# Attention values one tile later than their scores, side work a tile later, and ScalarE's waits in another order

## What is computed

```python
xq = _ada_ln(x_q, t_vec, Wss_q, bss_q)
xkv = _ada_ln(x_kv, t_vec, Wss_kv, bss_kv)
q = (xq @ Wq + bq).reshape(B, Lq, nh, dh)
kv = (xkv @ Wkv + bkv).reshape(B, Lkv, 2, nh, dh)
scores = jnp.einsum('bqhd,bkhd->bhqk', q, k) / jnp.sqrt(jnp.float32(dh))
attn = jax.nn.softmax(scores, axis=-1)
out = jnp.einsum('bhqk,bkhd->bqhd', attn, v).reshape(B, Lq, H)
return x_q + (out @ Wp + bp)
```

## Time and profile before

| what | value |
|---|---|
| median of 3 runs | 2179.65 us (2179.39 to 2180.37) |
| the profiled execution's own time | 2177.47 us |
| its span | 2175.8 us |
| TensorE clock granted | full in all slices |
| busy: TensorE, VectorE, ScalarE | 99%, 88%, 84% of the span |
| chain that ended last | TensorE 98%: scores 40%, values 37%, output 4%, queries 4%, keys and values of the context 8% |
| first key matmul, first scores, last values | 21.3, 226.1, 2151.5 us |

### The profile page before, as it was taken

The page is one execution under the profiler, slowest core; times in us unless marked ns, Lnnn a source line. Parts: engine busy times, 40 slices in busy tenths (PEclk is TensorE's granted clock), DMA queues, the critical chain, the costliest instruction groups (busy, mean ns, idle before and its releaser), DMA issues.

```text
span 2175.8 us, 56101 instructions
## 1 busy us (share of the span) xinstructions
PE 2149.7 (99%) x24986; PEld 620.3 (29%) x24986; DVE 1913.9 (88%) x1179; ACT 1819.8 (84%) x1940; POOL 17.3 (1%) x28
## 2 busy tenths in 40 slices
PE   7999999999999999999999999999999999999998
PEld 3444322222222222222222222222222222222222
DVE  2435798899999999999999999999999999999998
ACT  1221899999999999999999999999999999999995
POOL 0001000000000000000000000000000000000000
PEclk9999999999999999999999999999999999999999
DMA  8345521234222422233223322233222322242211
GB/s 299 141 166 180 160 75 55 77 90 117 70 81 73 135 69 77 64 99 109 81 71 99 107 81 70 77 99 104 69 81 89 99 74 77 70 118 80 77 54 51
DMA packets 189010, 210.22 MB, mean 97 GB/s; under 512 B 17238, under 2 KB 120414, under 8 KB 188764
## 3 DMA queue, kind: packets, MB, share of 16 engines
q1 hardware_dynamic: 187180, 206.06, 32.3%
q10 hardware_dynamic: 1584, 0.53, 0.1%
HBM read 169.33 MB, written 37.22 MB: 95 GB/s over the span
## 4 chain that ended last, share of the span: by engine, by line
PE 98%; DVE 1%; DMA 0%; issue 0%; ACT 0%; POOL 0%; SPq 0%; DVEq 0%
PE bank L1091 40%; PE bank L1103 37%; PE bank L1171 4%; PE bank L1120 4%; PE bank L1009 4%; PE bank L1020 4%; PE bank L1133 1%; PE bank L1146 1%; PE bank L1229 1%; PE bank L989 1%; DVE stats L1442 0%; PE bank L1156 0%; DVE arena L1456 0%; DMA arena<-in_ctx_dram 0%; POOL rstd L936 0%
## 5 line engine op out<-in xcount | busy, mean ns | idle before, releaser
L1340 ACT ACTIVATE arena<-bank,shift 128x1024 f32<-128x1024 f32 x1600 | 1693.7, 1115 | 151.3 <-PE bank L1091 146.3
L1650 DVE TENSOR_TENSOR arena<-arena 128x2048 f32<-128x2048 f32 x736 | 1658.4, 2288 | 110.8 <-ACT arena L1340 103.2
L1091 PE MATMUL bank<-qs,ks 32*64 32x512 f32 x12800 | 934.5, 613 | 1.1 <-ACT arena L1301 0.7
L1103 PE MATMUL bank<-arena,vg 128*32 128x512 f32 x6400 | 852.3, 605 | 1.3 <-ACT arena L1340 1.3
L1091 PEld LDWEIGHTS bank<-qs,ks 32*64 32x64 f32 x12800 | 213.8, 129 | 379.0 <-ACT arena L1340 197.9
L1103 PEld LDWEIGHTS bank<-arena,vg 128*32 128x32 f32 x6400 | 125.9, 108 | 650.6 <-ACT arena L1340 649.8
L1171 PE MATMUL bank<-wp,arena 128*32 128x168 f32 (+2 forms) x2464 | 153.6, 321 | 0.0
L1120 PE MATMUL bank<-xt,wq 128*32 128x256 f32 x1792 | 137.7, 379 | 0.0
L1171 PEld LDWEIGHTS bank<-wp,arena 128*32 128x32 f32 x2464 | 80.1, 110 | 184.4 <-issue 162.2
L1301 ACT ACTIVATE arena<-bank,bk_c 128x512 f32<-128x512 f32 (+1 forms) x28 | 18.0, 642 | 129.9 <-PE bank L1009 129.9
L1120 PEld LDWEIGHTS bank<-xt,wq 128*32 128x32 f32 x1792 | 58.2, 110 | 134.1 <-issue 118.2
(11 more groups left out here) (88 smaller groups left out, 424.2 us busy)
## 6 DMA issues: line engine op xcount, KB each, us to landing
ks<-k_full SPq DMA_DIRECT2D x160, 320.0 KB, 3.1
vg<-v_full SPq DMA_DIRECT2D x160, 320.0 KB, 3.9
p_b<-p_tails SPq DMA_DIRECT2D x128, 128.0 KB, 4.1
arena<-in_x_dram SPq DMA_DIRECT2D x13, 1024.0 KB, 8.1
q_full<-qs SPq DMA_DIRECT2D x32, 256.0 KB, 2.1
out_dram<-arena SPq DMA_DIRECT2D x32, 256.0 KB, 2.0
arena<-l_recip SPq DMA_DIRECT2D x28, 256.0 KB, 5.8
arena<-in_ctx_dram SPq DMA_DIRECT2D x6, 1024.0 KB, 13.5
```

The lines of the kernel that those rows point to most:

```text
L1091: mm = nc.tensor.matmul(bank[out, 2 * (i % RING) + h % 2, :], ks[rows_of(h), keys], qs[rows_of(h), g, :], start=True, stop=True)
L1103: mm = nc.tensor.matmul(bank[rows_of(h), o_bank(u), :], vg[:, t, rows_of(h)], pt[t % PR][:, h, :], start=(t == 0), stop=False, skip_group_ ...
L1340: nc.scalar.activation(pt[t % PR][:, 2 * pair:2 * pair + 2, :], bank[:, first:first + 2, :], ACT.Exp, scale=SCALE, bias=shift[:, g:g + 1]) ...
L1650: nc.vector.tensor_tensor(a[:, :, :], (pt[t - 1] if k <= 2 else a)[:, :, :], pt[t % PR][:, :, :], ALU.add).then_inc(p_added, 1)
```

## The change

On TensorE the values are one tile later: after scores(t + 1) come values(t - 1). The last tile's values come behind the loop, or, between units, behind the next unit's second scores block. All side pieces are a tile later on TensorE, so are the steps of ScalarE that take them, take_sums, and VectorE's inversion, division and residuals that follow. The last output piece of g = 0 is taken in tile 0 of the next unit. In `weights` the wait for s_ready stands first. At the start the first 512 context rows are loaded by four transfers with a semaphore each, VectorE waits for each tile by itself, and the bias of the modulation has a semaphore for each of its two halves.

```diff
-                    load_ctx(0)
+                    for j in range(TPB):
+                        sp.dma_start(cin[0][:, j, :], ctx2[j * P:(j + 1) * P, :]).then_inc(first_in[j], 16)
...
                     def first_side(u, b, t):
                         if b > 0:
-                            if 1 <= t < 5:
-                                project_queries(u, b, 3, 0, t - 1)
+                            if 2 <= t < 6:
+                                project_queries(u, b, 3, 0, t - 2)
...
                     def later_side(u, b, g, t):
                         if b > 0:
-                            if 1 <= t < 5:
-                                output(u, b - 1, g, 0, t - 1)
+                            if 2 <= t < 6:
+                                output(u, b - 1, g, 0, t - 2)
...
-                            weigh(u, t)
+                            if t > 0:
+                                weigh(u, t - 1)
+                            elif u > 0:
+                                weigh(u - 1, NT - 1)
                             if g == 0:
                                 first_side(u, b, t)
                             else:
                                 later_side(u, b, g, t)
+                    weigh(UNITS - 1, NT - 1)
...
                         b, g = divmod(u, NG)
+                        act.wait_ge(s_ready, items(u) + 2 * t + 1)
                         if NT * u + t - PR >= 0:
                             act.wait_ge(pv_done, NT * u + t - PR + 1)
...
-                            act.wait_ge(s_ready, n + 1)
+                            if pair == 1:
+                                act.wait_ge(s_ready, n + 1)
...
                             weights(u, t)
-                            if t < 2 and u > 0:
-                                take_sums(u - 1, t)
+                            if g == 1 and b > 0 and t == 0:
+                                take_output(u - 1, b - 1, 0, 1)
+                            if 1 <= t < 3 and u > 0:
+                                take_sums(u - 1, t - 1)
                             if g == 0:
-                                if b > 0 and t == 5:
+                                if b > 0 and t == 6:
                                     take_queries(u, b, 3, 0)
...
                     def statistics(src, tiles, n):
                         for j in tiles:
+                            if n == 0:
+                                dve.wait_ge(first_in[j], 16)
...
-                        dve.wait_ge(bss_in, 16 * 2 * HG)
+                        dve.wait_ge(bss_in[w], 16 * HG)
...
-                            if t == 10:
+                            if t == 11:
                                 invert(b - 1, NH)
-                            if t == 14:
+                            if t == 15:
                                 divide(b - 1, NG)
...
-                        if b > 0 and t == (3 if g == 1 else 17):
+                        if b > 0 and t == (3 if g == 1 else 18):
```

More of the change, by code:

```diff
@@ L164, in attention @@
             cond_in = sem("cond_in")
-            bss_in = sem("bss_in")
+            bss_in = [sem(f"bss_in{i}") for i in range(2)]
+            first_in = [sem(f"first_in{j}") for j in range(TPB)]
             bp_in = sem("bp_in")
@@ L1178, in first_side @@
                         if b > 0:
-                            if 1 <= t < 5:
-                                project_queries(u, b, 3, 0, t - 1)
[L1181 to L1191, removed]
+                            if 2 <= t < 6:
+                                project_queries(u, b, 3, 0, t - 2)
+                            if 6 <= t < 8:
+                                denominators(u, u - 1, t - 6)
+                            if 8 <= t < 12:
+                                project_queries(u, b, 3, 1, t - 8)
+                            if 17 <= t < 21:
+                                output(u, b - 1, 0, 0, t - 17)
+                            if 21 <= t < 25:
+                                output(u, b - 1, 0, 1, t - 21)
+                        if b + 1 < NB and t in (12, 14, 15, 16):
+                            turn_queries(u, b + 1, max(t - 13, 0))
+                        if t == 13:
                             tail_scores(u, b)
@@ L1195, in later_side @@
                         if b > 0:
-                            if 1 <= t < 5:
-                                output(u, b - 1, g, 0, t - 1)
[L1198 to L1203, removed]
+                            if 2 <= t < 6:
+                                output(u, b - 1, g, 0, t - 2)
+                            if 8 <= t < 12:
+                                output(u, b - 1, g, 1, t - 8)
+                            if 12 <= t < 16:
+                                output(u, b - 1, g, 2, t - 12)
+                        if 6 <= t < 8:
+                            denominators(u, u - 1, t - 6)
                         if b + 1 < NB:
[L1205 to L1208, removed]
+                            if 16 <= t < 20:
+                                project_queries(u, b + 1, g - 1, 0, t - 16)
+                            if 20 <= t < 24:
+                                project_queries(u, b + 1, g - 1, 1, t - 20)
                     pe.wait_ge(fills, 1)
@@ L1266, in _ @@
                                           bias[c * HB:(c + 1) * HB].rearrange("(a n) -> a n", a=1)
-                                          .broadcast_to([DH, HB])).then_inc(bss_in, 16)
+                                          .broadcast_to([DH, HB])).then_inc(bss_in[w], 16)
                     act.dma_start(bk_c[:, :], bkv[0:H].rearrange("(t p) -> p t", p=P),
@@ L1394, in _ @@
                                     take_queries(u, b, 3, 0)
-                                if b > 0 and t == 7:
+                                if b > 0 and t == 8:
                                     take_denominators(u, u - 1)
-                                if b > 0 and t == 11:
+                                if b > 0 and t == 12:
                                     take_queries(u, b, 3, 1)
-                                if b + 1 < NB and t == 12:
+                                if b + 1 < NB and t == 13:
@@ L1400, in _ @@
                                     modulate_queries(u, b + 1, 0)
-                                if t == 13:
+                                if t == 14:
                                     take_tail(u, b)
-                                if b + 1 < NB and 14 <= t < 17:
-                                    modulate_queries(u, b + 1, t - 13)
-                                if b > 0 and t == 20:
+                                if b + 1 < NB and 15 <= t < 18:
+                                    modulate_queries(u, b + 1, t - 14)
@@ L1406, in _ @@
+                                if b > 0 and t == 21:
                                     take_output(u, b - 1, 0, 0)
-                                if b > 0 and t == 24:
-                                    take_output(u, b - 1, 0, 1)
                             else:
-                                if b > 0 and t == 5:
+                                if b > 0 and t == 6:
                                     take_output(u, b - 1, g, 0)
-                                if t == 7:
+                                if t == 8:
@@ L1413, in _ @@
                                     take_denominators(u, u - 1)
-                                if b > 0 and t == 11:
+                                if b > 0 and t == 12:
                                     take_output(u, b - 1, g, 1)
-                                if b > 0 and t == 15:
+                                if b > 0 and t == 16:
                                     take_output(u, b - 1, g, 2)
-                                if b + 1 < NB and t == 19:
+                                if b + 1 < NB and t == 20:
@@ L1419, in _ @@
                                     take_queries(u, b + 1, g - 1, 0)
-                                if b + 1 < NB and t == 23:
+                                if b + 1 < NB and t == 24:
                                     take_queries(u, b + 1, g - 1, 1)
@@ L1464, in prepare @@
                             dve.wait_ge(x_in, 16)
-                        else:
-                            dve.wait_ge(c_in[c % 2], 16 * (c // 2 + 1) + (16 if c == KB - 1 else 0))
+                        elif c > 0:
+                            dve.wait_ge(c_in[c % 2], 16 * ((c + 1) // 2) + (16 if c == KB - 1 else 0))
                         n = NORM["s", s]
@@ L1618, in later_side @@
                     def later_side(b, g, t):
-                        if b > 0 and t == (3 if g == 1 else 17):
+                        if b > 0 and t == (3 if g == 1 else 18):
                             add_residual(b - 1, 0 if g == 1 else g)
-                        if b > 0 and g == 1 and t == 17:
+                        if b > 0 and g == 1 and t == 18:
                             add_residual(b - 1, 1)
```

## The result

The changed kernel takes 2162.28 us (median of 4 runs, 2160.16 to 2165.90) against 2179.52 us of the kernel before, run beside it (2177.10 to 2180.37): ratio 0.9924, 95% interval 0.9907 to 0.9942. The forecast was 2161.7, in a range of 2155 to 2171. The profiled execution has a span of 2159.6 us, 16.2 less than before.

What follows compares the result with a forecast made beforehand. TensorE, busy 99% of the span, was taken as the bound, its scores blocks stalled 43.3 us. 15.8 + 1.8 + 0.4 = 18.0 off 2177.5 gives 2159.5; with 2.2 for the median, 2161.7, range 2155 to 2171.

Steps and rivals of the forecast that it cites:

- What the values' wait costs: Values waiting for their tile's second exponential, in the loop: the wait costs nothing, so taking it away gains 0.
- The scores' stall and its condition: Scores blocks held when a step is under 2.37 us, for the first exponential before: 43.3 us stall, 15.8 gained.
- The order of the waits: ScalarE's waits before the exponentials: the step needed to avoid a hold falls from 2.37 to 2.29 us, by .08.
- The ends of the loop: One values block moves to where TensorE waits for the last exponentials: 0.4 us gained, bounds 0 to 1.0.
- The start: First context load in four parts: three of four statistics lie beside the transfer, 1.8 us gained, bounds 0.4 to 3.
- The sum: Scores' stall, start and loop ends together: 15.8 + 1.8 + 0.4 = 18.0 us off the profiled execution.
- VectorE did not take over: Rival in the loop: VectorE holds ScalarE and half the loop's gain is lost, 2170 us; chance .10.
- The slower rival: At unit starts TensorE, running ahead, waits for the sums' bank: 31 units lose 66 us, 2228; chance .04.
- The cheaper change of shape: Rival at 799 changes from scores to values: .12 us falls away at each, 96 us, giving 2066; chance .02.

Runs made afterwards that it cites:

- the order alone: The kernel before with only the order of ScalarE's waits changed, s_ready first: ratio 0.9932, span 2160.0 us.
- The later tiles with the old order: The changed kernel with s_ready back as the last of ScalarE's waits: ratio 1.0001 to the kernel before, span 2177.6 us.
- two more waits: The kernel before with two long-satisfied waits added behind s_ready, before each tile's first exponential (bar the first unit's first tiles): ratio 1.0057, span 2187.5 us.
- the start alone: The kernel before with only the four loads of the first context rows and the split semaphores: ratio 0.9999, span 2176.2 us.
- two queues: The changed kernel with every second part of the first context load issued by ScalarE: ratio 0.9935 to the kernel before, span 2159.3 us.

## Why the prediction was right, point by point

*What the values' wait costs: nothing.* Shown. Taking it away left the values block 1.05 behind the scores.

*The scores' stall and its condition.* Shown in both directions. The predicted 15.8 us were 14.9 in the changed kernel and 15.9 with the order alone. By blocks: middle 10.1 predicted, 10.3 measured; last 2.8 and 2.8; block 0 2.9 predicted, 2.8 with the order alone and 1.9 in the changed kernel. So the order gave what was predicted in block 0 too, and the later values took .9 of it back, for which the prediction had no term. It happens at the loop's start, in the changed kernel and then with the order alone:

```profile
228.03 3.10 PE L1093 MATMUL bank<-qs,ks 32*64 32x512 f32 x24 [0.43 <-ACT arena L1348]
...
228.28 1.09 PE L1091 MATMUL bank<-qs,ks 32*64 32x512 f32 x8 [0.43 <-ACT arena L1342]
230.29 1.11 PE L1091 MATMUL bank<-qs,ks 32*64 32x512 f32 x16
```

In the changed kernel no values block stands yet between the second half of one scores block and the next block, and the exponentials hold that next block: 24 records take 3.10 us instead of the 1.09 + 1.11 = 2.20 of the order alone, where a values block fills the time between. The later tiles with the old order show the same .9 (935.4 against 934.5).

*The order of the waits.* That the wait written first goes with the ACTIVATE was read from two lines' event counts, and holds. The step of .08 was right: 1.24 to 1.16. The Trainium skill, in Perfetto Trace Analysis, Identifying Dependency Chains, says that instructions which wait on several engines may have EventSemaphore instructions ahead of them. The traces agree: 797 such events on line 1339 before, 640 and 155 on lines 1339 and 1337 in the changed kernel, twice 795 with two more waits. What one costs behind the last arrival is the measured .08 for the first and .04 for the second.

*The ends of the loop: .4.* The loop is 16.2 shorter in the changed kernel, of which 14.9 is the scores' group. The other 1.3 is TensorE's wait for the last exponentials: 1.3 us stood before the values, .1 is left. With the .9 lost at the loop's start the later tiles bring only .2 against the order alone. Behind the loop .4 were given back: TensorE waits 1.41 us for VectorE's last additions, where it waited .96.

```profile
2142.70 1.07 PE L1247 MATMUL bank<-arena,ones 128*32 128x512 f32 x8 [1.41 <-issue]
```

*The start: 1.8.* This term was mis-sized; it measured .4. The statistics of the changed kernel show why:

```profile
4.12 0.69 DVE L1452 BATCH_NORM_STATS2 stats<-arena 128x6 f32<-128x512 f32 x1 [0.17 <-DMA arena<-in_ctx_dram]
5.19 0.69 DVE L1452 BATCH_NORM_STATS2 stats<-arena 128x6 f32<-128x512 f32 x1 [0.37 <-DMA arena<-in_ctx_dram]
7.68 1.30 DVE L1452 BATCH_NORM_STATS2 stats<-arena 128x6 f32<-128x512 f32 x2 [1.79 <-DMA arena<-in_ctx_dram]
```

Two of the four lay beside the transfer, not three. The third part was there .7 later than the whole load before, and the last landed at 8.3 against 7.0: the three further issues pushed it back by 1.3, near their own 3 x .49. That was the condition of the term's lower bound, .4, and .4 was what came. The modulation matmuls, expected near 15.1, began at 16.39.

*The sum.* 15.8 + 1.8 + .4 = 18.0 predicted, 16.2 measured between the profiled executions: the start was 1.4 too high, and the give-back behind the loop, .4, was not in the sum; the loop came out as predicted, 16.2. The forecast of the median is closer than its parts. It put 2.2 us between the profiled execution and the median, as before; that is about the distance between executions of the kernel before at a full and at a lower mean clock (last section). But in the changed kernel that distance is .9, and these 1.3 cancel most of the 1.8 by which the profiled execution was missed. With runs up to 3.6 us from their median, the closeness of 2161.7 to 2162.28 is largely luck.

*The rivals.* VectorE did not take over: of ScalarE's 137.7 us idle before exponentials, 135.2 ended with TensorE's scores. The side piece at a unit's start loads its weights .25 after the sums are out (827.01 + .38 = 827.39 against 827.64), the same as before. The slower rival's margin did not shrink, because side piece and sums were moved together and the scores ahead of both still wait for the first exponential. The cheaper change of shape did not come. The Trainium skill, in TensorEngine Tiling (Array Packing), Key Properties, says that a change of tiling mode drains TensorE, and the trace agrees: the values begin 1.05 behind the scores with 2.41 us to spare.

## What to carry to other kernels

Where two engines hand tiles to each other through a short ring, a few hundredths of a microsecond between an arrival and the start of the work that waited for it are paid again in each tile where TensorE is held by that start: here .08 us, and in many tiles less than that, came to 16 us over 800 tiles. Look whether the wait that comes last in time sits with the instruction or on an event ahead of it, and write that wait first. And before a dependency is loosened, compare starts with and without it: the name in the bracket of a wait column can be that of something long done.

## What had not been expected

TensorE's granted clock at the start is not the same in every execution. In the two profiles whose first eight key matmuls took 5.2 to 5.4 us, the stretch from 21 to 25 us has a granted clock of 0.67 and 0.62, a mean over times at 2.4 and at 1.2 GHz; the others have 1.00. Of the start alone, in stretches 17 to 21, 21 to 25 and 21 to 23, where the clock is at the lower level throughout:

```profile
17.00:21.00 4.00, 2.14 (x29) 1.32 (x22) 0.66 (x3) 1.30 (x2) 0.00 (x0) 0.91 1.08 366
21.00:25.00 4.00, 4.00 (x7) 1.67 (x7) 1.13 (x2) 1.48 (x3) 0.00 (x0) 0.67 1.04 402
21.00:23.00 2.00, 2.00 (x3) 0.76 (x3) 0.00 (x0) 1.48 (x3) 0.00 (x0) 0.50 1.06 396
```

TensorE had been busy for 2.14 of the 4 us before 21. But the changed kernel and the one with two queues have 2.14 there too and kept their clock, so what decides it stays open. It is worth 1.5 to 1.7 us in these eight matmuls, as much as the whole gain that the start was to bring. In the same two profiles the modulation matmuls took 2.48 and 2.98 us instead of 1.93, although the granted clock reads 1.00 up to 19 us; why is open too.

The kernel before has it both ways as well. Of its 13 executions beside four of the experiments, the whole change except the order among them, seven have a mean granted clock of 1.000 and take 2177.35 to 2178.24 us, six have 0.999 and take 2179.53 to 2180.43. This also bears on the whole change except the order. Its three executions at 1.000 take 2175.86 to 2176.65 us, some 1.5 below the seven, so the 1.8 by which its profiled execution was longer goes with the clock at the start and not with the change.
